# The projection by wo in high and low fp32r parts, contexts in two places, and a spread tail

## The reference

```python
def _L0_xattn_ref(q_x, k_x, v_x, energy_coeffs, Wq, bq, Wk, bk, Wv, bv, Wo, bo):
    Q = (q_x @ Wq + bq)...; K = (k_x @ Wk + bk)...; V = (v_x @ Wv + bv)...   # 16 heads of 32
    scores = einsum('bhqd,bhkd->bhqk', Q, K) / sqrt(32) * gate[:, None, None, :]
    attn = softmax(scores)
    out = einsum('bhqk,bhkd->bhqd', attn, V)
    return out @ Wo + bo
x = x + tanh(g_xattn) * _L0_xattn_ref(layernorm(x), ctx, ctx, ctxb, ...)
x = x + tanh(g_ffn) * _L0_ffn_ref(layernorm(x), ...)    # 2 shared experts, 2 of 16 routed ones
```

## Time and profile before

| what | value |
|---|---|
| median of 3 runs | 2010.88 us (2009.51 to 2011.35) |
| the profiled execution | 2016.03 us, span 2014.3 us |
| TensorE busy | 1921.4 us, 95% of the span |
| GpSimd, VectorE, ScalarE busy | 61%, 55%, 39% |
| mean granted clock of TensorE | 0.98 of full speed |

### The profile page before, as it was taken

One profiled execution on the slowest core, in us unless ns is written; L12 is line 12 of the kernel. 1 busy time (PEld: TensorE's weight loads), 2 busy tenths in 40 slices (PEclk: granted clock), 3 DMA queues, 4 the chain that ended last, 5 costly groups with the idle time before them and its releaser, 6 DMA issues. The chain is left out here.

```text
span 2014.3 us, 40479 instructions
## 1 busy us (share of the span) xinstructions
PE 1921.4 (95%) x12469; PEld 1495.3 (74%) x12470; DVE 1109.4 (55%) x1765; ACT 784.2 (39%) x1557; POOL 1221.2 (61%) x1383
## 2 busy tenths in 40 slices
PE   6899999999999999999999999998879899999798
PEld 5687877878777787877878787786658766666587
DVE  4566565655656566565656556565347533333277
ACT  3345454444545444454444545444432122222000
POOL 2367677776867777676776867775522433332462
PEclk9899999999999999999999999999889999999799
DMA  7763837557493754838466483756144454444786
GB/s 211 207 164 110 249 99 202 141 151 202 112 242 102 186 155 134 234 99 220 118 174 167 131 243 100 198 143 180 50 161 166 164 159 143 148 141 131 206 239 205
DMA packets 171274, 331.82 MB, mean 165 GB/s; under 512 B 20294, under 2 KB 69446, under 8 KB 170582
## 3 DMA queue, kind: packets, MB, share of 16 engines
q1 hardware_dynamic: 154316, 285.79, 49.8%
q0 software_dynamic: 10800, 33.30, 6.0%
q10 hardware_dynamic: 6112, 12.13, 1.8%
HBM read 214.83 MB, written 115.80 MB: 164 GB/s over the span
## 5 line engine op out<-in xcount | busy, mean ns | idle before, releaser
L946 DVE TENSOR_REDUCE neg_max<-score 112x1 f32<-112x750 f32 x508 | 476.6, 938 | 552.0 <-PE score L1255 550.4
L652 ACT ACTIVATE probs_t<-st_pair 125x448 f32<-125x448 f32 x768 | 413.8, 541 | 503.1 <-PE st_pair L1281 500.2
L521 POOL TENSOR_TENSOR acc<-acc,probs_t 125x448 f32<-125x448 f32 x256 | 309.1, 1208 | 54.1 <-ACT probs_t L652 52.9
L1281 PE MATMUL st_pair<-q_stack,k_stack 98*125 98x224 f32 x1536 | 330.5, 297 | 1.7 <-ACT probs_t L652 1.3
L1216 PE MATMUL proj<-ctx_hi,weights 128*128 128x376 f32 (+1 forms) x1024 | 329.0, 346 | 0.0
L523 POOL TENSOR_TENSOR acc<-acc,probs_t 125x448 f32<-125x448 f32 x256 | 295.0, 1152 | 20.1
L1281 PEld LDWEIGHTS st_pair<-q_stack,k_stack 98*125 98x125 f32 x1536 | 265.9, 188 | 53.9 <-issue 23.5
L1255 PE MATMUL score<-k_stack,q_stack 96*112 96x512 f32 x1016 | 282.2, 359 | 19.5 <-DMA k_stack<-k_parts 10.2
L1226 PE MATMUL proj<-weights,ctx_hi 128*125 128x512 f32 x768 | 248.6, 405 | 2.2 <-issue 2.2
L513 POOL TENSOR_TENSOR acc<-probs_t 125x448 f32<-125x448 f32 x128 | 145.7, 1140 | 169.2 <-PE pv L1334 152.7
L1255 PEld LDWEIGHTS score<-k_stack,q_stack 96*112 96x112 f32 x1016 | 159.3, 178 | 71.7 <-issue 48.6
(11 more groups left out here) (241 smaller groups left out, 2764.4 us busy)
## 6 DMA issues: line engine op xcount, KB each, us to landing
k_stack<-k_parts SPq DMA_DIRECT2D x192, 375.0 KB, 6.4
ctx_raw<-in_ctx_t SPq DMA_DIRECT2D x64, 375.0 KB, 10.2
k_parts<-k_hi SPq DMA_DIRECT2D x64, 375.0 KB, 6.4
k_parts<-k_lo SPq DMA_DIRECT2D x64, 375.0 KB, 7.1
y_slots<-y_sb SPq DMA_DIRECT2D x71, 256.0 KB, 3.0
q_stack<-q_parts SPq DMA_DIRECT2D x64, 224.0 KB, 4.8
gu_sb<-in_w_gu ACTq DMA_DIRECT2D x4, 2048.0 KB, 15.2
x_in<-in_x SPq DMA_DIRECT2D x16, 448.0 KB, 9.3
```

The source lines that it names most:

```text
L521: nc.gpsimd.tensor_tensor(both, both, tiles(c, p, pair, 0), ALU.add).then_inc(half_added, 1)
L652: act.activation(probs_t[0:KW, (c * PHASES + p) % 2, u % HC, :], st[u % 2][0:KW, 0:2 * L], ACT.Exp)\
L946: nc.vector.tensor_reduce(neg_max[:, h // HC % 2, h % HC, t:t + 1], score_place(b, h, t)[0:QW, 0:S], axis=AX.X, op=ALU.max, negate=True).t ...
L1281: ins = nc.tensor.matmul(st[u % 2][0:KW, k * L:(k + 1) * L], k_stack[0:SHIFTED, h, kt * KW:(kt + 1) * KW], q_stack[0:SHIFTED, h, :], start ...
```

## The change

It has four parts.

1. `project_out`: chunks 0 to 2 of the attention output and of wo are split into a high and a low fp32r part, so each is three fp32r matmuls instead of one fp32 matmul; chunk 3 stays fp32. ScalarE and VectorE make the parts of the output (`output_high`, `output_low`) in every batch, and those of wo (`wo_high`, `wo_low`) once, in batch 0.
2. `ctx_raw` has two places instead of four. The loads of d = 2 and 3 are issued after the stack load of chunk 3, and each waits for the remainder of the chunk whose place it takes. ScalarE converts after the exponentials 4, 6, 9 and 11, and VectorE's remainder of d = 1 stands one maximum earlier. For the first batch d = 2 and 3 go to a spare part of the probabilities.
3. In the final block light group 1's load and gathers move from before the first heavy group into the second round, and TensorE's four groups are a hardware loop.
4. The shared experts' weights are loaded in two transfers to two places; the space for the gathers' descriptors is 4096 instead of 8192 bytes.

```diff
+SPLIT_O = 3
...
-        ctx_raw = sb("ctx_raw", [P, DC, S])
+            gu_second = last_use.enter_context(nc.sbuf_tensor("gu_second", [P, DC // 2, 2 * MID_S], F32))
+        ctx_raw = sb("ctx_raw", [P, 2, S])
+        fresh = sb("fresh", [P, 2, HALF_K[0]])
...
+        wo_lo = sb("wo_lo", [P, SPLIT_O, D], F32R)
+        if SPLIT_O < DC:
+            sb("wo_rest", [P, DC - SPLIT_O, D])
+        wo_hi = sb("wo_hi", [P, SPLIT_O, D], F32R)
...
+        def raw(n, d):
+            return raw_spare[:, d - 2, :] if isinstance(n, int) and n == 0 and d >= 2 else ctx_raw[:, d % 2, :]
...
-                sp.dma_start(ctx_raw[:, d, :],
+                sp.dma_start(raw(n, d),
                              ctx_t[bass.ds(n, 1), :, d, :].rearrange("a p s -> p (a s)")).then_inc(raw_in[d], 16)
 
             def reload_raw(n, d):
-                sp.wait_ge(ctx_lo_done[d % 2], (n - 1) * 2 + d // 2 + 1)
+                sp.wait_ge(ctx_lo_done[d % 2], n * 2 + d // 2)
                 load_raw(n, d)
...
-                    for d in range(DC):
+                    for d in (0, 1):
                         reload_raw(n, d)
...
+                if not last:
+                    for d in (2, 3):
+                        reload_raw(n, d)
...
+            def output_high(b, c):
+                act.wait_ge(normed, b * DC + c + 1)
+                act.activation(out_hi[:, c, :], out_t[:, c, :], ACT.Copy).then_inc(out_hi_done, 1)
+
+            def wo_high(c):
+                act.activation(wo_hi[:, c, :], wo_sb[:, c, :], ACT.Copy).then_inc(wv_hi_done, 1)
...
-                    if not last and u in (4, 6, 7, 8):
-                        ctx_high(n, (4, 6, 7, 8).index(u), b)
+                    if not last and u in (4, 6, 9, 11):
+                        ctx_high(n, (4, 6, 9, 11).index(u), b)
+                    if first and u in (1, 2, 10):
+                        wo_high((1, 2, 10).index(u))
...
+                    if u == 1:
+                        output_high(b, 0)
...
+            def output_low(b, c):
+                dve.wait_ge(out_hi_done, b * SPLIT_O + c + 1)
+                nc.vector.tensor_tensor(out_lo[:, c, :], out_t[:, c, :], out_hi[:, c, :].bitcast(F32), ALU.subtract)\
+                    .then_inc(out_lo_done, 1)
+
+            def wo_low(c):
+                dve.wait_ge(wv_hi_done, DC + c + 1)
+                nc.vector.tensor_tensor(wo_lo[:, c, :], wo_sb[:, c, :], wo_hi[:, c, :].bitcast(F32), ALU.subtract)\
+                    .then_inc(wv_lo_done, 1)
...
+                if not first:
+                    output_low(b - 1, 2)
+                else:
+                    wo_low(0)
                 next_maximum(b, 7, 1)
                 if not first:
                     normalize_output(b - 1, 3, base)
+                else:
+                    wo_low(1)
                 next_maximum(b, 8, 0)
+                if not last:
+                    ctx_remainder(n, 1)
                 next_maximum(b, 8, 1)
-                if not last:
-                    ctx_remainder(n, 1)
                 shift_low(b, 1, b)
                 next_maximum(b, 9, 0)
...
-                    if t == 0:
+                    if t == 0 and c < SPLIT_O:
+                        pe.wait_ge(out_lo_done, m * SPLIT_O + c + 1)
+                    elif t == 0:
                         pe.wait_ge(normed, m * DC + c + 1)
-                    ins = nc.tensor.matmul(bank[0:QW, :], out_t[:, c, t * QW:(t + 1) * QW], wo_sb[:, c, :],
-                                           start=(c == 0), stop=(c == DC - 1))
+                    terms = ((out_hi, wo_hi), (out_hi, wo_lo), (out_lo, wo_hi)) if c < SPLIT_O else ((out_t, wo_sb),)
+                    for k, (op, wp) in enumerate(terms):
+                        ins = nc.tensor.matmul(bank[0:QW, :], op[:, c, t * QW:(t + 1) * QW], wp[:, c, :],
+                                               start=(c == 0 and k == 0), stop=(c == DC - 1 and k == len(terms) - 1))
...
-            for l in range(RING):
-                load_light(l)
+            load_light(0)
             for s in range(HEAVY):
+                if s == 1:
+                    load_light(1)
...
-                for l in range(RING) if s == 0 else range(RING + s - 1, min(RING + s, HEAD)):
+                for l in ((0,), (1, 2), (3,), ())[s]:
...
-            for g in range(HEAVY):
+            with pe.Fori(0, HEAVY) as g:
...
-                   dynamic_dma_scratch_size=8192)
+                   dynamic_dma_scratch_size=4096)
```

More of the change, by code:

```diff
@@ L104, in attention_phase @@
         wk_hi, wk_lo, wv_hi, wv_lo = (weights[:, i, :].rearrange("p (c n) -> p c n", c=DC) for i in range(4))
+        with ExitStack() as last_use:
+            gu_first = last_use.enter_context(nc.sbuf_tensor("gu_first", [P, DC // 2, 2 * MID_S], F32))
         wq_sb = sb("wq_sb", [P, DC, D])
@@ L129, in attention_phase @@
         v_sb = sb("v_sb", [P, KT, D])
-        wo_sb = sb("wo_sb", [P, DC, D])
+        with ExitStack() as unsplit:
+            wo_sb = unsplit.enter_context(nc.sbuf_tensor("wo_sb", [P, DC, D], F32))
+        wo_lo = sb("wo_lo", [P, SPLIT_O, D], F32R)
+        if SPLIT_O < DC:
+            sb("wo_rest", [P, DC - SPLIT_O, D])
+        wo_hi = sb("wo_hi", [P, SPLIT_O, D], F32R)
         probs_t = sb("probs_t", [P, 2, HC, 2 * L])
@@ L135, in attention_phase @@
         xn_t = sb("xn_t", [P, DC, L])
-        out_t = sb("out_t", [P, DC, L])
+        with ExitStack() as unsplit:
+            out_t = unsplit.enter_context(nc.sbuf_tensor("out_t", [P, DC, L], F32))
+        out_lo = sb("out_lo", [P, SPLIT_O, L], F32R)
+        if SPLIT_O < DC:
+            sb("out_rest", [P, DC - SPLIT_O, L])
+        out_hi = sb("out_hi", [P, SPLIT_O, L], F32R)
         rw_sb = sb("rw_sb", [P, DC, E_R])
@@ L239, in attention_phase @@
         normed = sem("normed")
+        out_hi_done = sem("out_hi_done")
+        out_lo_done = sem("out_lo_done")
         res_ready = sem("res_ready")
@@ L264, in pieces, with gu_raw @@
             return b * PIECES + h * QT + t
+        def raw(n, d):
+            return raw_spare[:, d - 2, :] if isinstance(n, int) and n == 0 and d >= 2 else ctx_raw[:, d % 2, :]
+        def gu_raw(c):
+            return gu_first[:, c, :] if c < DC // 2 else gu_second[:, c - DC // 2, :]
         def score_place(b, h, t):
@@ L411, in batch @@
                     sp.wait_ge(proj_done[bank_of(b, "V5")], turn_of(b, "V5") + 1)
[L412 removed]
+                    sp.dma_start(gu_first[:, :, :], ws_gu[:, 0:DC // 2, :]).then_inc(shared_in, 16)
+                    sp.dma_start(gu_second[:, :, :], ws_gu[:, DC // 2:DC, :]).then_inc(shared_in, 16)
                 if not first:
@@ L498, in ctx_remainder @@
                 pool.wait_ge(ctx_hi_done, n * DC + d + 1)
-                remainder(ctx_lo[:, d, :], ctx_raw[:, d, :], ctx_hi[:, d, :]).then_inc(ctx_lo_done[d % 2], 1)
+                remainder(ctx_lo[:, d, :], raw(n, d), ctx_hi[:, d, :]).then_inc(ctx_lo_done[d % 2], 1)
             def key_low(n, name):
@@ L665, in shared_high @@
                 if i < DC:
-                    act.wait_ge(shared_in, 16)
-                    act.activation(shared["gu_hi"][:, c, :], gu_raw[:, c, :], ACT.Copy).then_inc(shared_hi, 1)
-                else:
-                    act.wait_ge(shared_in, 32)
+                    act.wait_ge(shared_in, 32)
+                    act.activation(shared["gu_hi"][:, c, :], gu_raw(c), ACT.Copy).then_inc(shared_hi, 1)
+                else:
+                    act.wait_ge(shared_in, 48)
+                    act.wait_ge(shared_lo, DC)
                     act.activation(shared["d_hi"][:, c, :], d_raw[:, c, :], ACT.Copy).then_inc(shared_hi, 1)
@@ L807, in batch @@
                     exponential(b, 3, u)
+                    if u == 2:
+                        output_high(b, 1)
+                    if u == 10:
+                        output_high(b, 2)
                     if last and u == 1:
@@ L904, in shared_low @@
                 dve.wait_ge(shared_hi, i + 1)
-                lo, raw, hi = (shared["gu_lo"], gu_raw, shared["gu_hi"]) if i < DC else (shared["d_lo"], d_raw, shared["d_hi"])
-                nc.vector.tensor_tensor(lo[:, c, :], raw[:, c, :], hi[:, c, :].bitcast(F32), ALU.subtract)\
+                lo, full, hi = (shared["gu_lo"], gu_raw(c), shared["gu_hi"]) if i < DC else (shared["d_lo"], d_raw[:, c, :], shared["d_hi"])
+                nc.vector.tensor_tensor(lo[:, c, :], full, hi[:, c, :].bitcast(F32), ALU.subtract)\
                     .then_inc(shared_lo, 1)
@@ L1047, in batch @@
                 next_maximum(b, 9, 1)
+                if not first:
+                    add_result(b, 1, b - 1)
+                else:
+                    wo_low(2)
                 if not last:
                     ctx_remainder(n, 3)
-                if not first:
-                    add_result(b, 1, b - 1)
                 if last:
@@ L1083, in batch @@
                 next_maximum(b, 13, 1)
+                output_low(b, 0)
                 next_maximum(b, 14, 0)
```

(5 more changed lines are left out.)

15 lines of the change are left out of this document (6 added, 9 removed).

## The result

The changed kernel takes 2061.05 us in the median of 4 runs (2050.78 to 2065.35), the kernel before 2011.01 (2009.51 to 2011.35): ratio 1.0245, 95% interval 1.022 to 1.0271. It is **slower by 50 us**; the forecast was 8.6 us slower (2019.5), with a range from 1984 to 2052. The profiled execution of the changed kernel is its fastest (2050.78), that of before 5 us above its median, so the two traces lie only 34.7 us apart. Stages are cut at the first exponential of each batch and at the end of the last wo matmul; the last column is the prediction's term.

A forecast was written before the change was run, and what follows sets the result against it. TensorE, 95% busy, was taken as the bound, with GpSimd nearly critical at sum_up(b, 0). Terms +19.6 + 2.0 + 0 - 1.0 - 12 = +8.6 us on the median 2010.88 gave 2019.5 us, range 1984 to 2052.

The forecast's parts named there:

- Part 2, the contexts: Attention loop, batches 1 to 14: a later d=2 load delays GpSimd and sum_up(b, 0) by 1.4 us per batch, +19.6 us.
- The chain of five instructions: In each batch: place_shift's DMAs, exponential 9, d=2 conversion, GpSimd's second remainder (2.77 us late), then the sum 1.4 us later.
- Part 1: Projection by wo: cheaper matmuls save 1.0 us per batch; the added copies and subtractions cost 0 on idle ScalarE and VectorE.
- The clock rival: Attention batches: TensorE's new gap drops its clock, 3.0 us lost in three batches of four, +31, 2051 us; chance 0.16.
- Batch 0: First attention batch: wo's split +1.2 us, the later contexts +0.8, together +2.0 (0 to 4).
- Part 3, -12 us: Final block: fewer gathers and loads ahead of the first heavy group shorten its stall, -12 us (-18 to +3).
- its own test: Final block, profile after: the first group should stand near 37 us, against 49 before.
- the stall that stays or moves: Final block rival: gather count is not the cause, or the stall moves to a later group; -12 gone, 2031.5 us; chance 0.09.
- wo's saving: Projection by wo: 1.0 us saved per batch, 0.2 lost at once, so TensorE reaches the sum 0.8 us earlier.

The follow-up runs named there:

- f7: The kernel before with only the contexts in two places and the shared weights' two transfers; wo and final block as before: 2029.84 us, ratio 1.0099.
- e1: The changed kernel with ScalarE's output_high(b, 0) moved to after column 1's last exponential: 2027.65 us, ratio to before 1.0188.
- e3: The changed kernel with output_high(b, 0) after column 1's last exponential and GpSimd's d=2 remainder one pair of additions later: 1991.05 us, ratio to before 0.9994.
- second pair: Traces of f5 (before) and f6 (changed), a second set beside the first traces of both kernels; span 60.3 us longer after, against 34.7 in the first.
- f5: The kernel before, unchanged, run and traced again: 2008.07 us, ratio to other runs of the same kernel 1.0006.
- f6: The changed kernel, unchanged, run and traced again: 2060.99 us, ratio to before 1.0252; its trace is the slowest run, 2067.19.
- g9: e3's kernel with, in batch 0 alone, wo's split in column 3 and VectorE's d=1 remainder behind reduction (8, 1): 1993.96 us, ratio to before 0.9934.
- e2: The changed kernel with GpSimd's context remainder for d=2 one pair of additions later in its queue: 2014.61 us, ratio to before 1.0122.

## Why the prediction was wrong, point by point

- **Part 2, the contexts: right in the loop.** The chain of five instructions came within 0.05 us each, and in the full kernel its share of the loop is 14 x 1.44 = 20.2 us (forecast 19.6; its last sum, 532.37 + 2.05 + 0.05, is 534.47 and not 534.45, which changes nothing). That f7 alone measured +22 against 20.4 is partly luck: its one trace has 5.1 us in batch 0 for the 0.8, and long remainders and a lower clock that the forecast does not have.
- **Part 1, "the added halves ... I take 0, with 0 to 0.3 us per batch as bounds": the step that failed.** The argument was from busy shares, 39% and 55%. The price was not in the 0.38 us of the copy or the 0.39 of the subtraction but in where they stand: VectorE waits 3.74 us in batch 5, in front of a reduction that TensorE needs. TensorE's gap behind it is 1.16 us or more in every batch. In quiet batches the way from sum 0 to sum 1 is 22.56 - 21.11 = 1.45 us longer, 14 x 1.45 = 20.3 us in the loop, and e1 and e3 take it away by moving one ScalarE instruction.
- **The clock rival: a share of it.** I had it as a case of its own (3.0 us in three batches of four, +31). It came on top of the forecast, in four or five batches of 14 at 1.7 us: 6.8 to 8.5 us. The remaining difference of the loop in the second pair is -2.9 us (46.1 - 20.2 - 20.3 - 8.5). It lies behind sum 1 (2.0 us up to sum 2, 0.7 behind that); TensorE waits 6.4 us for `k_stack` in f5 and 4.6 in f6, which may be part of it.
- **Batch 0: "I take 1.2 us" for wo's split, +2.0 in all: mis-sized**, +6.5 and +10.6. 3.4 us of each is time lost to the clock. In f6, as in e3, TensorE waits 4.77 us behind the remainder for d=1, and g9 shows that VectorE's additions to batch 0 make this wait. In the first trace that remainder took 1.99 us, and TensorE's longest gap of the batch, 3.05 us, is for ScalarE's `x_in`; what made that one was not tested.
- **Part 3, -12 us: mis-sized, though its own test came true.** The first group takes 37.3 us as forecast, but the block alone moves the time by +2.4 and -2.8 us only (by the ratios). The stall of the first group was read as a loss that ends with the gathers; in two of the nine traces the second group stalls as long as the first. The -12.4 reads as a hit in the first pair of traces and is luck: one execution against another, +3.7 in the second pair. The prediction had this as its rival, the stall that stays or moves, at 0.09.
- **wo's saving: right where it arises, half of it kept.** The projection ends 0.75 us earlier (0.8 forecast), but without the gaps only 0.3 to 0.4 us are left at the sum: a wait for VectorE's reduction on the way takes part of it.

Put together: 20.2 + 20.3 + 8.5 - 2.9 in the loop (the second pair's), 6.5 to 10.6 in batch 0 and about 0 at the end are 53 to 57, against 50.0 and 53.6 between the medians.

## What to carry to other kernels

When a change adds an operation to an in-order queue, look up both ends of it: where its input is produced on the other engine's queue, and what stands behind it on its own. A producer placed after work that runs later than the consumer's place is a wait, however idle both engines are on average. And do not book a gain in a stage whose length differs between executions from one trace; runs of that part alone, timed against before, would have shown it to be within a few us of zero.

## What the runs showed that was not expected

- VectorE's remainder for d=1 (128 x 750, fp32r from fp32) took 0.93 us in every loop batch of before. Beside GpSimd's work on the same chunks it took 1.62 us in twelve of the fourteen loop batches of after, 2.74 in batches 1 and 13, and 4.80 in batch 0 of e3. In batch 13 this delays place_shift, the conversion and GpSimd's second remainder by 1.1 us (it starts at 18.73 us of the batch instead of 17.62) and the sum by 0.8. VectorE in batches 12 and 13 of after, and GpSimd in batch 0 of e3:

```profile
1163.35 1.62 DVE L941 TENSOR_TENSOR parts<-ctx_raw,ctx_hi 128x750 fp32r<-128x750 f32 x1
```

```profile
1254.49 2.74 DVE L941 TENSOR_TENSOR parts<-ctx_raw,ctx_hi 128x750 fp32r<-128x750 f32 x1
```

```profile
87.16 0.20 POOL L520 TENSOR_TENSOR neg_mean<-zeros,neg_mean 112x2 f32<-112x2 f32 x1
87.32 1.14 POOL L539 TENSOR_TENSOR acc<-probs_t 125x448 f32<-125x448 f32 x1
88.42 1.76 POOL L502 TENSOR_TENSOR parts<-ctx_raw,ctx_hi 128x750 fp32r<-128x750 f32 x1
90.14 1.12 POOL L547 TENSOR_TENSOR acc<-acc,probs_t 125x448 f32<-125x448 f32 x1
91.34 1.70 POOL L549 TENSOR_TENSOR acc<-acc,probs_t 125x448 f32<-125x448 f32 x1
```

  VectorE's remainder there starts at 87.26, while GpSimd's short instruction of 87.16 runs, and ends at 92.06, 0.80 us after the addition of 90.14 has ended at 91.26. In batches 12 and 13 of after it also starts while a GpSimd instruction runs, and ends 0.78 and 0.80 us after the end of that one and of the next one. By the Trainium skill, "SBUF — State Buffer", section "SBUF: two separate sides", a VectorE operation with two SBUF inputs and a GpSimd operation that reads SBUF take turns at a shared pair of ports: whichever starts first holds it for its whole instruction, and the other is blocked. The trace agrees that VectorE waits for the end of a GpSimd instruction, but in e3 it lost to the three that followed as well. Which engine goes next differs between batches that look alike: in f7 the remainder starts at 12.4 to 12.5 us of the batch each time, and takes 2.02 us in twelve batches and 0.94 in two.

- In the loop the clock falls behind TensorE's gaps, and without them it never falls (eight traces). All 23 falls in six traces follow a gap of 1.47 to 1.84 us: 17 the first one, 6 the second, which is 1.16 us in most batches and 1.4 to 1.8 in some; none comes right behind a gap of 1.16. With the second gap alone (e2) the loop loses 1.7 us, with the first alone 6.8 (e1) and 8.5 (f7), with both 6.8 to 8.5. Why the second gap grows in some batches was not looked into.
- The kernel before has more than one level on one chip: 1991.1 us (23 runs) and 2007.4 (13 runs) in two series.
